# Local transformers of a fused network: order of the transfers on the sync queue, and the projection weights loaded in parts

## The reference, cut to what matters

```python
def local_attention(q, k, v):          # windows of 32 tokens, each sees itself and the one before
    sim = jnp.einsum('bhwie,bhwje->bhwij', bq, bk2) * QK_SCALE
    attn = jax.nn.softmax(jnp.where(mask, -max, sim), -1)
    return jnp.einsum('bhwij,bhwje->bhwie', attn, bv2)

def attn_layer(x, Wqkv, qs, ksc, Wo):  # 16 heads of 64
    q, k, v = jnp.split(x @ Wqkv, 3, -1)     # Wqkv: 128 x 3072
    q, k = rotary(l2norm(q) * qs), rotary(l2norm(k) * ksc)
    return merge(local_attention(q, k, v)) @ Wo      # Wo: 1024 x 128

for i in range(6):
    x = attn_layer(shift_tokens(x), Wqkv[i], ..., Wo[i]) + x
    x = ffn_layer(shift_tokens(x), ..., W1[i], b1[i], W2[i], b2[i]) + x
```

## Time and profile before

| | |
|---|---|
| median of 3 runs | 4618.58 us (4618.03 to 4622.97) |
| the profiled execution's own time | 4620.06 us |
| its span, first to last instruction | 4618.3 us |
| PE busy | 4008.3 us, 87% of the span |
| DVE, ACT, POOL busy | 3666.2, 3352.4, 3330.8 us (79%, 73%, 72%) |
| mean granted TensorE clock | 0.935 of full speed |
| local transformers | about 558 to 2225 us and 2501 to 4167 us of the span |

### The profile page before, as it was taken

One profiled execution on the slowest core, in us unless ns is written; L12 is line 12 of the kernel. 1 busy time (PEld: TensorE's weight loads), 2 busy tenths in 40 slices (PEclk: granted clock), 3 DMA queues, 4 the chain that ended last, 5 costly groups with the idle time before them and its releaser, 6 DMA issues. The chain is left out here.

```text
span 4618.3 us, 128913 instructions
## 1 busy us (share of the span) xinstructions
PE 4008.3 (87%) x47211; PEld 2598.8 (56%) x47211; DVE 3666.2 (79%) x7231; ACT 3352.4 (73%) x10612; POOL 3330.8 (72%) x4118
## 2 busy tenths in 40 slices
PE   5888789999999999999503999999999999995675
PEld 2222256666666666667301666666666666663353
DVE  5999878788887888877596888888888888865657
ACT  4666478899898989989201898889989888882121
POOL 1777588888888888887365888888888888861313
PEclk7999999999999999999756999999999999997787
DMA  1000100101101011010001011111111111110000
GB/s 26 0 0 0 43 22 23 52 23 36 38 23 52 23 48 27 23 39 23 10 0 43 23 30 45 30 41 28 43 32 30 46 27 30 27 30 3 5 3 9
DMA packets 69295, 121.54 MB, mean 26 GB/s; under 512 B 24872, under 2 KB 46052, under 8 KB 67172
## 3 DMA queue, kind: packets, MB, share of 16 engines
q1 hardware_dynamic: 68708, 113.70, 9.4%
HBM read 35.56 MB, written 1.05 MB: 8 GB/s over the span
## 5 line engine op out<-in xcount | busy, mean ns | idle before, releaser
L933 POOL TENSOR_TENSOR local_qk<-local_qk,local_rb 128x512 f32<-128x512 f32 x768 | 975.2, 1276 | 280.6 <-DVE local_rb L1327 280.0
L1207 ACT ACTIVATE local_pr<-local_tb,local_nmax 128x96 f32<-128x96 f32 x3072 | 1008.6, 383 | 42.2 <-DVE local_nmax L1339 42.2
L1029 PE MATMUL local_pj<-local_wqkv,local_xs 128*128 128x512 f32 x1536 | 851.9, 638 | 32.2 <-DVE local_rb L1327 20.3
L939 POOL TENSOR_TENSOR local_qk<-local_qk,local_rinv 128x512 f32<-128x512 f32 x768 | 784.7, 1043 | 7.5
L1207 ACT ACTIVATION_READ_ACCUMULATOR local_pr<-local_tb,local_nmax 128x1 f32 x3072 | 765.1, 250 | 0.0
L955 POOL TENSOR_TENSOR local_pr<-local_pr,local_rsum 128x384 f32<-128x384 f32 x768 | 630.2, 826 | 150.0 <-DVE local_rsum L1345 149.9
L1324 DVE TENSOR_TENSOR local_qk<-local_pj,local_rope 128x512 f32<-128x512 f32 x768 | 525.5, 684 | 73.1 <-ACT local_sq L1190 34.5
L1190 ACT ACTIVATE local_sq<-local_pj 128x512 f32<-128x512 f32 x768 | 460.6, 600 | 164.3 <-PE local_pj L1029 134.4
L1334 DVE TENSOR_REDUCE local_ss<-local_sq 128x8 f32<-128x512 f32 x768 | 519.4, 677 | 20.2 <-ACT local_sq L1190 19.5
L1327 DVE TENSOR_TENSOR local_rb<-local_pj,local_rope 128x512 f32<-128x512 f32 x768 | 523.5, 682 | 9.7 <-POOL local_qk L933 9.7
L1215 ACT ACTIVATE local_prT<-local_tb 128x512 f32<-128x512 f32 x768 | 454.0, 606 | 73.0 <-PE local_tb L1067 73.0
(11 more groups left out here) (383 smaller groups left out, 7877.6 us busy)
## 6 DMA issues: line engine op xcount, KB each, us to landing
local_v<-local_v SPq DMA_DIRECT2D x288, 256.0 KB, 4.0
local_wqkv<-L_ffn_Wqkv_dram SPq DMA_DIRECT2D x12, 1536.0 KB, 7.7
local_wo<-L_ffn_Wo_dram SPq DMA_DIRECT2D x12, 512.0 KB, 5.1
local_w<-L_ffn_W_dram SPq DMA_DIRECT2D x12, 341.0 KB, 3.0
mamba_parts<-mamba_in_low SPq DMA_DIRECT2D x12, 128.0 KB, 2.3
local_w<-L_ffn_W_dram SPq DMA_DIRECT2D x12, 128.0 KB
y_dram<-store_xtok SPq DMA_DIRECT2D x4, 256.0 KB, 2.5
local_oT<-rope_dram SPq DMA_DIRECT2D x2, 256.0 KB, 2.8
```

The source lines that it names most:

```text
L933: nc.gpsimd.tensor_tensor(qk[:, u, :], qk[:, u, :], rb[:, u % 2, :], ALU.add).then_inc(s["summed"], 1)
L939: nc.gpsimd.tensor_tensor(heads8(qk[:, u, :]), heads8(qk[:, u, :]), r, ALU.mult).then_inc(s["scaled"], 1)
L1029: nc.tensor.matmul(bank[:, :], xs[:, par, u // 4 * P:(u // 4 + 1) * P], wqkv[:, dep % 2, u % 4 * BANK:(u % 4 + 1) * BANK], start=True, sto ...
L1207: ins = nc.scalar.activation(pr[:, (NU * c + k) % PR_RING, i, WIN:WIN + KW], scores[:, i * KW:(i + 1) * KW], ACT.Exp, bias=nmax[:, k, i:i ...
```

## The change

Two things change, both in SP's list. First, `move_v` is issued ahead of `next_wo`. Second, every load of wqkv is cut into six parts of 512 columns (128 x 512, 256 KB). In the pipeline, the six parts are issued in six successive steps, the first in the step of the old whole load; in the prefetch and ahead of the pipeline the six stand behind each other. Each of the two wqkv buffers has its own semaphore now, and PE waits for six parts of the layer's buffer.

```diff
+        WPARTS = 6
+
+        def load_wqkv(sp, k, part):
+            own = slice(part * BANK, (part + 1) * BANK)
+            sp.dma_start(wqkv[:, k % 2, own], d["L0_ffn_Wqkv"][k][:, own]).then_inc(s[f"wqkv_in{k % 2}"], 16)
...
-            sp.dma_start(wqkv[:, 0, :], d["L0_ffn_Wqkv"][0]).then_inc(s["wqkv_in"], 16)
+            for part in range(WPARTS):
+                load_wqkv(sp, 0, part)
...
             def next_wqkv(a, par, _):
-                k = a // B
-                if a % B == B - 1 and k + 2 < DEPTH:
+
+                k, part = (a + 1) // B - 1, (a + 1) % B
+                if k >= 0 and k + 2 < DEPTH and part < WPARTS:
                     sp.wait_ge(s["projected"], QK_UNITS * (a + 1))
                     sp.wait_ge(s["v_projected"], V_UNITS * (a + 1))
-                    sp.dma_start(wqkv[:, k % 2, :], d["L0_ffn_Wqkv"][k + 2]).then_inc(s["wqkv_in"], 16)
+                    load_wqkv(sp, k + 2, part)
...
                 run(next_w2, 5, 0)
+                run(move_v, 3, 0)
                 run(next_wo, 4, 0)
-                run(move_v, 3, 0)
-
-            sp.wait_ge(s["wqkv_in"], 16)
-            sp.dma_start(wqkv[:, 1, :], d["L0_ffn_Wqkv"][1]).then_inc(s["wqkv_in"], 16)
+
+            sp.wait_ge(s["wqkv_in0"], 16 * WPARTS)
+            for part in range(WPARTS):
+                load_wqkv(sp, 1, part)
...
-                pe.wait_ge(s["wqkv_in"], 16 * (a // B) + 16)
+                dep = a // B
+                pe.wait_ge(s[f"wqkv_in{dep % 2}"], 16 * WPARTS * (dep // 2 + 1))
```

More of the change, by code:

```diff
@@ L736, in local_transformer @@
         rope0 = oT_flat[:, QKS:QKS + 2 * 4 * DH].rearrange("p (t a c) -> p t a c", t=2, a=4)
-        s = {n: net.sem(f"{tag}_{n}") for n in "wqkv_in wo_in w1_in w2_in cols_in const_in".split()}
+        s = {n: net.sem(f"{tag}_{n}") for n in "wqkv_in0 wqkv_in1 wo_in w1_in w2_in cols_in const_in".split()}
+        WPARTS = 6
+        def load_wqkv(sp, k, part):
+            own = slice(part * BANK, (part + 1) * BANK)
+            sp.dma_start(wqkv[:, k % 2, own], d["L0_ffn_Wqkv"][k][:, own]).then_inc(s[f"wqkv_in{k % 2}"], 16)
         def load_wo(sp, k):
@@ L890, in iteration @@
                 run(next_w2, 5, 0)
+                run(move_v, 3, 0)
                 run(next_wo, 4, 0)
-                run(move_v, 3, 0)
-            sp.wait_ge(s["wqkv_in"], 16)
-            sp.dma_start(wqkv[:, 1, :], d["L0_ffn_Wqkv"][1]).then_inc(s["wqkv_in"], 16)
+            sp.wait_ge(s["wqkv_in0"], 16 * WPARTS)
+            for part in range(WPARTS):
+                load_wqkv(sp, 1, part)
             pipeline(sp, iteration)
-            sp.wait_ge(s["wqkv_in"], 16 * DEPTH)
+            for i in range(2):
+                sp.wait_ge(s[f"wqkv_in{i}"], 16 * WPARTS * DEPTH // 2)
             for i in range(2):
```

## The result

The changed kernel takes 4565.19 us (median of 4 runs, 4562.73 to 4568.42) against 4618.31 us (4615.79 to 4622.97, 4 runs) for the kernel before: a ratio of 0.9884, 95% interval 0.9867 to 0.9901. It is faster by 53.1 us, where the forecast was 45.5 (4618.6 - 4573.1). The forecast range began at 4568, so the kernel is faster than its lower end. The mechanism was the forecast one, its size was not.

What follows compares the result with a forecast made beforehand. PE bounds each step, plus ten waits at layer changes. Span 4618.3 - 46.95 (waits and slow clock) + 1.5 (prefetch) = 4572.85 us; plus 1.76 for the execution's own time, less 1.48 to the median: 4573.1, range 4568 to 4583.

Steps and rivals of the forecast that it cites:

- What bounds the kernel, and what PE waits for: Local transformers: PE alone sets step time; before `weigh` at ten layer changes it waits 30.3 us for late value moves.
- The moves ahead of wo: At ten layer changes, issuing the moves before the wo load saves idle time and the slow clock after it: 46.95 us.
- The prefetch: Before each local transformer, five more issues ahead of the block's end barrier cost 1.5 us, bounds 0 and 4.5.
- Stages outside: Stages outside the local transformers: no saving or cost entered in the sum, apart from the prefetch's 1.5 us.
- One part ahead of the moves in six steps: In six steps per layer, a wqkv part before the moves costs 0, hidden by 4.1 us of other work.
- the assumed price with the cover gone: If a wqkv part lost all its 4.1 us of cover: 0.9 us in each of 48 steps.
- The room at the other end: A layer's last wqkv part goes out two steps before its first `project`, some 40 us.
- The fixed cost that the Trainium skill gives to each DMA: Rule against six wqkv loads: about 2.0 us per DMA, 80 us in all if exposed, 4653 us; unchanged behind cover.
- (B): At layer changes, the wo load shares engines with the moves and still delays them: 6.5 us, 4579.6 us; chance 0.08.
- (C): At layer changes, PE's wait is for something other than the moves, so time stays at 4620 us; chance 0.04.
- (D): In 48 steps, wqkv parts delay the moves: 43 us, or 67 with the lower clock, 4640 us; chance 0.04.

Runs made afterwards that it cites:

- the filler: The kernel before plus three unneeded products that PE does at each layer change while it waits for the late moves: 4599.04 us, ratio 0.9956.
- the kernel without cover: The changed kernel, but each wqkv part waits until the values are written and so is issued right ahead of the moves: 4568.36 us, ratio 0.9888.

## Why the prediction was right or wrong

*What bounds the kernel, and what PE waits for*: right. PE alone counts in a step, and the ten waits are for the moves, which stood behind the wo load and its wait. They are gone, and in the profile with the filler the moves are named as the releaser.

*The moves ahead of wo*: right in kind, and the step that failed is its size, "What is saved is ... 46.95 us". The waits themselves are 30.2 to 32.5 us in all five profiles of the old order (with an eleventh, short one in four of them). What follows them is not a constant: the loops took 46.3, 51.9, 51.5, 51.9 and 50.4 us more than the 3107.8 of the new order. I counted in one profile, the lowest of these, and gave the range no room for it. The term measured 50.4, 3.5 us more: the waits took 31.3 in place of 30.3, and the slower clock about 19 in place of the 16.6 (ten times 1.66), since it stayed at its lower level for 47.8 us in the other profiles and for 37.5 in the one that I read.

*The prefetch*: the 1.5 us are wrong, it is 0. In the changed kernel SP's first six small loads took 5.77 us in place of 9.44: the time in which SP stood there took in all five added issues. The lower bound of 0 was the truth, and the prediction had named the reason without giving it enough weight.

*Stages outside*: the prediction took them as unchanged. The dense stage is another 2.7 us shorter on average, in five profiles against three; that the change brings this isn't shown. 3.5 + 1.5 + 2.7 is 7.7, the 53.1 - 45.5 = 7.6 us by which the forecast gain was too small.

*One part ahead of the moves in six steps*: right at cost 0, and more strongly than argued: the assumed price with the cover gone (0.9 us a step) is wrong as well, no wait came of it. The room at the other end was larger than said, too: the first layer's last part was issued at 1007.6 us and the first `project` that reads it started at 1084.3, 77 us later and not some 40. The fixed cost that the Trainium skill gives to each DMA ("DMA: Bandwidth & Descriptors", section "Anatomy of one DMA — SWDGE (gpsimd) path"), about 2.0 us, does not fall in full on what is queued behind it here: the moves right behind a part landed 1.0 us later on average, its issue included.

*Rivals*: (B), the wo load still in the moves' way, did not come: at the first layer change they land in 3.1 to 4.2 us, and no wait is left. (C) is refuted by the gain, (D) by the kernel without cover and by the one with the parts only. What none of them named was a gain above the forecast.

## What to carry to other kernels

In a queue that one engine issues in order, a wait for a late event holds every transfer behind it. Put the transfers whose users come soonest ahead of loads that are needed a step later; it cost one swapped line and gave 1.2%. When such a stall ends on TensorE, price it by several profiles: its idle time, averaged over ten waits, repeated here to a few tenths of a microsecond (3.0 to 3.3), while the slower clock behind it cost 16 us in all in one profile and 19 to 20 in the others. Two delays that share one reserve must be removed or priced together, not one by one.

## What the runs showed of the hardware that I had not expected

Around a standstill of 2.3 to 4.1 us the granted clock fell in 55 of 60 cases and did not in five, in one pair for the same program and nearly the same idle time (3.03 and 3.02 us); standstills up to 1.7 us brought no fall. A fall lasted 3.4 or 6.8 us, and that mix was most of what made one profile of the same program differ from the next. Three products that nobody needs, done in the standstill, made the kernel 20 us faster. The dense stage took 234.3 to 234.8 us or 238.6 to 240.3, and which of the two went with whether the clock rose by 3.8 us behind its first product or later. And a transfer of 256 KB right in front of the moves put their last landing off by 1.0 us on average and by 1.4 at most.
